# Five phase blocks that end with the semaphore barrier alone, GpSimd's ring drain left out

## What is computed

```
x = layernorm(x + L0(x, edge_weight, src, dst))
x = layernorm(x + L1(x, edge_attr_64, src, dst))
L0: msgs = z[dst] @ Wd + z[src] @ Ws + w * ww + bm
    agg  = segment_max(msgs, dst)
    out  = relu(z @ W1a + agg @ W1b + b1) @ W2 + b2
L1: h = x @ node_fc_W + b;  a = sum(h[src] * h[dst]);  alpha = segment_softmax(a, dst)
    beta = segment_softmax of three gates that a small MLP makes of edge_attr_64
    segment sums of alpha * h[src] and beta * h[src], two projections, relu, gated mix
```

## Time and profile before

| | us |
|---|---|
| median of 3 runs | 2283.71 |
| fastest, slowest | 2282.62, 2285.59 |
| profiled execution, span from first to last instruction | 2723.8 |
| busy in it: PE, PEld | 1843.7, 1146.6 |
| busy in it: DVE, ACT, POOL | 1328.7, 1115.3, 1639.6 |

### The profile page before, as it was taken

One profiled execution on the slowest core, in us unless ns is written; L12 is line 12 of the kernel. 1 busy time (PEld: TensorE's weight loads), 2 busy tenths in 40 slices (PEclk: granted clock), 3 DMA queues, 4 the chain that ended last, 5 costly groups with the idle time before them and its releaser, 6 DMA issues. The chain is left out here.

```text
span 2723.8 us, 43235 instructions
## 1 busy us (share of the span) xinstructions
PE 1843.7 (68%) x9891; PEld 1146.6 (42%) x9891; DVE 1328.7 (49%) x5220; ACT 1115.3 (41%) x3305; POOL 1639.6 (60%) x1705
## 2 busy tenths in 40 slices
PE   4577777677767777655666766676776776766665
PEld 3122222222222222114355655565665665655565
DVE  3454555554444444324535544544544545445459
ACT  1233333333333333333544444444444444444448
POOL 3666666666767777646455655555565655555525
PEclk7689888888889888876867777777777777777788
DMA  8433333333333333323311221221112221211113
GB/s 228 144 120 124 109 116 118 125 109 109 121 109 114 101 123 110 124 80 87 116 46 47 54 51 48 52 51 49 51 51 50 53 52 49 52 48 50 49 44 119
DMA packets 115983, 235.04 MB, mean 86 GB/s; under 512 B 32909, under 2 KB 68230, under 8 KB 106422
## 3 DMA queue, kind: packets, MB, share of 16 engines
q0 software_dynamic: 52832, 109.39, 16.3%
q1 hardware_dynamic: 56522, 97.21, 9.7%
q10 hardware_dynamic: 6540, 27.42, 2.9%
HBM read 166.01 MB, written 67.89 MB: 86 GB/s over the span
## 5 line engine op out<-in xcount | busy, mean ns | idle before, releaser
L463 POOL DMA_INDIRECT d_region<-d_h,d_region x784 | 747.8, 954 | 534.2 <-issue 221.1
L209 POOL DMA_INDIRECT acc<-d_src_product,b_region x784 | 779.4, 994 | 378.6 <-issue 225.5
L651 PE MATMUL banks<-acc,b_region 64*128 64x512 f32 x1176 | 351.8, 706 | 213.9 <-ACT acc L756 99.4
L859 DVE SCALAR_TENSOR_TENSOR acc<-b_region,acc 128x128 f32<-128x128 f32 x784 | 271.4, 346 | 433.6 <-DMA acc<-d_src_product,b_region 416.8
L1577 DVE TENSOR_TENSOR acc<-acc,banks 128x160 f32 x784 | 252.5, 322 | 318.6 <-remote 124.0
L1376 PE MATMUL banks<-d_region 128*128 128x128 f32 x1568 | 306.0, 357 | 4.1 <-issue 3.8
L1379 PE MATMUL banks<-d_region,pick 128*128 128x128 f32 x1568 | 294.1, 346 | 11.6 <-issue 11.2
L651 PEld LDWEIGHTS banks<-acc,b_region 64*128 64x128 f32 x1176 | 109.8, 211 | 429.7 <-issue 188.3
L1379 PEld LDWEIGHTS banks<-d_region,pick 128*128 128x128 f32 x1568 | 277.4, 262 | 13.6 <-issue 13.4
L1376 PEld LDWEIGHTS banks<-d_region 128*128 128x128 f32 x1568 | 271.2, 260 | 10.3 <-issue 5.3
L870 DVE SCALAR_TENSOR_TENSOR acc<-acc,b_region 128x128 f32<-128x128 f32 x784 | 270.1, 345 | 7.5 <-remote 5.2
(11 more groups left out here) (261 smaller groups left out, 2450.3 us busy)
## 6 DMA issues: line engine op xcount, KB each, us to landing
d_runs<-acc SPq DMA_DIRECT2D x48, 1024.0 KB
acc<-ea ACTq DMA_DIRECT2D x25, 1024.0 KB
acc<-d_src_product,b_region POOLq DMA_INDIRECT x784
d_region<-d_h,d_region POOLq DMA_INDIRECT x784
d_region<-d_rel SPq DMA_DIRECT2D x49, 256.0 KB
hT<-xT SPq DMA_DIRECT2D x7, 448.0 KB, 6.9
d_src_product<-acc SPq DMA_DIRECT2D x7, 448.0 KB, 3.7
acc<-xrow SPq DMA_DIRECT2D x1, 3136.0 KB
```

The lines of the kernel that those rows point to most:

```text
L209: pool.indirect_dma_start(self.rows[:, s, j, :], None, d["B"], bass.IndirectOffsetOnAxis(self.idx[:, k:k + 1], 0)).then_inc(self.gathered[ ...
L463: pool.indirect_dma_start(rows[:, s, :], None, table, bass.IndirectOffsetOnAxis(idx[:, s:s + 1], 0)).then_inc(gathered[q], 16)
L651: last = nc.tensor.matmul(bank[4 + n % 2 * 2 + h][:, :], wf[h * DE:(h + 1) * DE, m * P:(m + 1) * P], ea[h * DE:(h + 1) * DE, u % (2 * UC), ...
L859: nc.vector.scalar_tensor_tensor(rows[:, s, j, :], wwb, wgt[:, k:k + 1], rows[:, s, j, :], ALU.mult, ALU.add).then_inc(ch, 1)
```

## The change

In all five phases the block is opened with a flag. The same line is changed at L249, L565, L985, L1256 and L1630:

```diff
@@ phase_tables
         ident, ones = t["ident"], ca(P)
-        block = ctx.enter_context(nc.Block())
+        block = ctx.enter_context(nc.Block(no_gpsimd_drain=True))
```

## The result

The changed kernel takes 2271.88 us (median of 6 runs, 2264.3 to 2279.13) against 2284.65 us for the kernel before (6 runs, 2282.62 to 2290.06). The ratio is 0.994 with a 95% interval of 0.9921 to 0.996, so 13.7 us faster by the ratio, between 9.1 and 18.0. The forecast of 2273.2 us lies 1.3 us from the median, and its ratio, 2273.2 / 2283.71 = 0.9954, inside the interval. One run, of 2329.21 us at a granted clock of 0.64, was left out of the ratio of experiment 9.

A forecast was written before the change was run, and what follows sets the result against it. The prediction took POOL's queue to bound B and C, with barriers between phases paid in full. Its terms, -8.4 (B) - 2.2 (A) + 0.1 (semaphores) = -10.5 us, took 2283.7 to 2273.2 us; range 2267.0 to 2282.0.

The forecast's parts named there:

- The mechanism: At block ends, POOL's drain counts only where it outlasts every other engine's arrival: gains at A and B, none elsewhere.
- Each sign that the prediction named for it: No POOL drain at block ends; release soon after the last arrival; C, D, E barriers and first-gather times unchanged.
- D's loop fetches nothing: Slower rival: shifted instruction streams make D's loop fetch a piece again each pass, 28 us more, 2301 us; chance 0.04.
- The term for the added semaphore operations: Added EVENT_SEMAPHOREs on PE, ACT, DVE and SP at block ends lengthen the path by 0.1 us.
- The term of A: End of A: without POOL's drain the release follows DVE's arrival, 2.2 us off the path.
- The third rival: End of A: if DVE's unexplained wait belongs to the profiler, the drain exposes 9 us, giving 2266.4 us; chance 0.11.
- The term of B: End of B: POOL arrives last, so without its drain the release comes 8.4 us earlier.
- The work comes back later: B's drain does bookkeeping over past DMAs that returns at C's first gathers; only A's gain stays, 2281.6 us; chance 0.13.
- The drain is short without the profiler: Unprofiled, B's drain may take 0.56 us instead of 8.4: 2281.0 us at best, 2283.2 without A's gain; chance 0.12.

The follow-up runs named there:

- experiment 9: Kernel before with one more GpSimd drain right behind the last gathers of B, all other drains kept: 2282.91 us, ratio 0.9964 to the kernel before.
- C, D, E: Kernel before with POOL's drain left out at the ends of phases C, D and E only: 2290.3 us, ratio 0.9998.
- A alone: Kernel before with POOL's drain left out at the end of A only, timed twice: 2276.33 us (ratio 0.9939) and 2277.18 us (0.9944).
- experiment 7: Whole change, but POOL waits at A's end until its 12 gathers for B have landed: 2284.11 us, ratio 0.9973 to the kernel before.
- the probes: Kernel before with two drains, then lots of landed gathers, each lot followed by a drain, added behind POOL's last wait in B; run once each for traces.
- the first experiment: The kernel before, unchanged, timed and profiled again: 2288.74 us, ratio 0.999, profiled span 2287.6 us.

## Why the prediction was right, and where its sum was wrong

**The mechanism held.** The gain sits at the barriers of A and B; C, D and E gave nothing (-0.5 us, interval -2.5 to 1.4), D's loop fetches nothing, and the first gathers of C are as quick as ever. Each sign that the prediction named for it is in the trace. The term for the added semaphore operations was small and still too small: the release stands 93 to 153 ns behind the last drain at A, C, D and E where it stood 26 to 44 behind, some 0.3 us in all and not 0.1.

**The term of A was mis-sized.** The "2.2 us off the path" at the end of A are 8.4 to 9.7 us in the six other executions that keep this drain. The failing step is the choice "I take 2.2, as the trace has it, since nothing shows that this wait is the profiler's". It wasn't the profiler's; it was that execution's. Nor was the pause as empty as the prediction took it: seven packets of POOL's queue still landed in it, the last at 63.0 us, too few to show in the 0.00 of the earlier trace rows. The third rival, "The drain exposes more at A", had the mechanism and nearly the price (9 us), with a chance of 0.11. A sign was on the page: a span 440 us above the median of the runs. A stretch that ends on a wait which no instruction released was not fit to be carried over at full length.

**The term of B was right alone and wrong in company.** "8.4 us off the path" was measured by itself as 8.0. But the change leaves out A's drain too, and with that gone B's is 1.87 us. The working treated the five drains as separate; they share one count.

**Two errors, partly cancelling.** The forecast lies 1.3 us from the measured median, and that is luck: A's drain exposes 7 us more than the sum took, and some 6 us come back in B, which the sum had at nothing. What the two drains hold is 9.4 us at A (the mean of the six traces) and 8.4 at B, 17.8 together, and 15.1 were measured. POOL pauses 3.41 to 3.54 us ahead of the scatter (L599) in the seven traces without a drain at A, 2.11 to 2.20 us in six with it (the execution of the earlier trace rows apart): 1.3 us, on the path. In the kernel before again:

```profile
1066.39 0.99 POOL L599 DMA_INDIRECT d_runs<-b_region  x1 [2.19 <-DVE b_region L942]
```

And VectorE's last step of B (L870) starts 1000.3 to 1004.4 us after the release in the seven, 995.4 to 999.5 in the six, 5.1 us more in the mean. With the 0.3 us of the semaphore operations that is 17.8 - 1.3 - 5.1 - 0.3 = 11.1. The profiled executions come near that: their spans are 2277.4, 2281.1 and 2281.4 us with the whole change, and 2287.6 and 2293.2 for the kernel before and for C, D, E, a difference of 10.4 in the means. (With A alone they are 2275.5 and 2277.4, so they scatter by a few us.) But each of those three is the longest of its six runs, 7 to 9 us above the median. The 15.1 us come from the other runs too, which left no trace, and where they gain the rest isn't known (the three intervals together reach from 9 to 20 us).

Why B's chain is longer without A's drain isn't known either. That the gathers land inside B is not the reason. In the kernel of experiment 7 they have landed before the release at 61.5 us, and its drain is gone; VectorE's last step (L872 there) and the scatter (L601) come as late as in the other kernels without the drain, 1004.1 us after the release and behind a pause of 3.50:

```profile
L872 DVE SCALAR_TENSOR_TENSOR acc<-acc,b_region x784: 337/347/401, 68.4 to 1065.6; 128x128 f32<-128x128 f32 x196
1073.15 1.00 POOL L601 DMA_INDIRECT d_runs<-b_region  x1 [3.50 <-issue]
```

So the difference goes with the drain, not with the landing. The 6.4 us that come back in B are near the 6.5 by which B's drain is shorter once A's is gone. That this work has moved into B would fit; no run tried it.

**The rivals.** "The work comes back later" was right that B's drain is bookkeeping over past DMAs. It had the place and the price wrong: the work doesn't return in C's first gathers. In the probes it returns at the 114th transfer, for a third of what the drain takes; in B no row gather shows a pause of that size, and how much of the 6.4 us that come back there is this work stays open. The argument against it, that a gather late in B takes 0.94 us and follows at 0.30, rested on one gather; a settlement that comes once in 113 can't be ruled out by one. "The drain is short without the profiler" falls with the first experiment. The page that the prediction weighed ("VectorE: DVE Perf Modes" of the Trainium skill, section "The DRAIN you can't avoid") gives about 12 ns for the boilerplate drains of a program's preamble and postamble, and says nothing of a drain at a block's end. POOL's drains here take 186 ns at the program's start, 46 ns right behind another drain, and 9266 ns behind 113 gathers. Nor are the other engines' all as short as the two that the prediction named: ACT's takes 962 ns at the end of A, and PE's 3453 at the end of C.

## What to carry to other kernels

A drain of GpSimd at a phase's end has two prices: it holds the barrier until everything that GpSimd issued has landed, also what only the next phase needs, and it settles past transfers, here up to 113 at 82 ns each. If it can't be left out, put one ahead of it where GpSimd waits anyway; when one drain is removed, expect the next one's length to change. Before carrying a term over from a profiled execution, set its span beside the unprofiled median, and distrust a cover that rests on a wait with no releaser.

## What was not expected of the hardware

- A drain of GpSimd with nothing in flight takes 37 ns and 82 ns for each indirect DMA (of 128 rows) since the last settlement, up to 113 (9266 ns), then falls to 119 ns at 114. A second drain right behind takes 46 ns.
- In the probes GpSimd's own settlement of 113 indirect DMAs takes one pause of 3.0 us between two issues. Among the row gathers of B there is no pause over 1.3 us.
- Behind 12 gathers that had not landed the drain ended 0.9 us behind the last landing (1606.8 to 1607.66 us), and at the end of A of the kernel before 1.2 us behind it (61.9 to 63.1).
- Two profiled executions of the kernel before took 2723.8 and 2287.6 us, with mean granted clocks in B and D of 0.86 and 0.76, and of 0.90 and 0.88.
